# Output projection of a fused attention and FFN kernel: bias rows through ScalarE instead of a matmul

## The reference, cut to what matters

```
x : [128, 64, 128]   ctx : [128, 64, 128]        (8192 tokens of width 128; 16 heads of width 8)
k = ctx @ Wk.T + bk ;  v = ctx @ Wv.T + bv ;  q = layernorm(x) @ Wq.T + bq
attn = softmax(k.q / sqrt(8)) over the 64 keys ;  out = attn applied to v
x = x + (out @ Wo.T + bo)                        # the output projection that is changed
h = layernorm(x)
3 times:  y = lin(gelu(layernorm(lin(h)))) ;  h = y + h      # dequantised weights plus low rank parts
x = x + h
```

## Time and profile before

| | |
|---|---|
| median of 3 runs | 371.1 us (370.62 to 373.37) |
| the profiled execution | 371.78 us |
| its span in the trace | 370.0 us, mean granted clock of TensorE 0.986 |
| instructions | 13066 |

### The profile page before, as it was taken

One profiled execution on the slowest core, in us unless ns is written; L12 is line 12 of the kernel. 1 busy time (PEld: TensorE's weight loads), 2 busy tenths in 40 slices (PEclk: granted clock), 3 DMA queues, 4 the chain that ended last, 5 costly groups with the idle time before them and its releaser, 6 DMA issues.

```text
span 370.0 us, 13066 instructions
## 1 busy us (share of the span) xinstructions
PE 342.1 (92%) x4797; PEld 256.4 (69%) x4797; DVE 334.4 (90%) x834; ACT 285.0 (77%) x575; POOL 268.6 (73%) x265
## 2 busy tenths in 40 slices
PE   7778999999999999999979785989999999999985
PEld 5355567677667766776756563776788888888874
DVE  5897999999999999999999999769999999988762
ACT  4567888788878878887867445558999999999983
POOL 4555678888877987788788878857787778784231
PEclk9989999999999999999999998799999999999999
DMA  7994476568547754864661400000011000100112
GB/s 191 245 275 135 135 233 205 156 183 244 175 134 213 211 162 139 253 194 144 176 198 73 131 4 2 3 0 0 3 31 58 28 28 28 59 29 30 57 31 85
DMA packets 54514, 43.29 MB, mean 117 GB/s; under 512 B 4608, under 2 KB 48592, under 8 KB 54480
## 3 DMA queue, kind: packets, MB, share of 16 engines
q1 hardware_dynamic: 53904, 42.31, 38.4%
q10 hardware_dynamic: 576, 0.53, 0.5%
HBM read 26.05 MB, written 16.78 MB: 116 GB/s over the span
## 4 chain that ended last, share of the span: by engine, by line
PE 65%; DVE 21%; issue 5%; ACT 5%; DMA 1%; POOL 1%; DVEq 0%; ACTq 0%; POOLq 0%
PE score_ps L1468 10%; DVE negmax L746 6%; PE att_ps L1444 6%; DVE zsum L760 6%; PE score_ps L1375 6%; PE wo_ps L1224 5%; PE score_ps L1236 4%; PE score_ps L1536 3%; PE work L1529 3%; PE work L1260 3%; PE att_ps L1536 3%; PE score_ps L1462 3%; PE work L1273 3%; PE work L1266 2%; PE work L1254 2%
## 5 line engine op out<-in xcount | busy, mean ns | idle before, releaser
L492 POOL TENSOR_TENSOR probs<-probs,rz 128x1024 f32<-128x1024 f32 x64 | 136.3, 2139 | 35.4 <-DVE rz L763 35.2
L503 POOL TENSOR_TENSOR rs<-ve,minus_half 128x4 f32<-128x4 f32 (+1 forms) x50 | 59.3, 1186 | 42.1 <-DVE ve L700 30.7
L1017 ACT ACTIVATE probs<-score_ps 128x1024 f32<-128x1024 f32 x64 | 65.6, 1024 | 22.9 <-PE score_ps L1375 22.4
L760 DVE TENSOR_REDUCE zsum<-probs 128x64 f32<-128x1024 f32 x64 | 77.3, 1208 | 1.5 <-ACT probs L1017 1.3
L746 DVE TENSOR_REDUCE negmax<-score_ps 128x64 bf16<-128x1024 f32 x64 | 75.2, 1177 | 1.7 <-PE score_ps L1236 1.7
L1375 PE MATMUL score_ps<-negmax,ident_bf 128*128 128x512 bf16 x128 | 39.2, 388 | 8.4 <-DVE negmax L746 8.3
L1468 PEld LDWEIGHTS score_ps<-lin_t,h 128*128 128x128 f32 x312 | 38.7, 195 | 11.7 <-DVE h L823 6.3
L1224 PEld LDWEIGHTS wo_ps<-wo_t,att_t 128*128 128x128 f32 x256 | 36.8, 191 | 13.7 <-issue 12.1
L1073 ACT ACTIVATE z<-score_ps,rs 128x128 f32<-128x128 f32 x156 | 44.7, 382 | 1.0 <-POOL rs L503 1.0
L1444 PE MATMUL att_ps<-probs,v_diag 128*32 128x64 f32 x2048 | 43.5, 224 | 0.7 <-POOL probs L492 0.6
L1468 PE MATMUL score_ps<-lin_t,h 128*128 128x128 f32 x312 | 41.6, 281 | 2.5 <-ACT probs L1017 1.1
(11 more groups left out here) (215 smaller groups left out, 680.9 us busy)
## 6 DMA issues: line engine op xcount, KB each, us to landing
q_parts<-parts SPq DMA_DIRECT2D x15, 512.0 KB, 3.5
k_stack<-k_parts SPq DMA_DIRECT2D x30, 256.0 KB, 3.3
q_stack<-q_parts SPq DMA_DIRECT2D x60, 128.0 KB, 2.8
ctx_sb<-in_ctx SPq DMA_DIRECT2D x16, 256.0 KB, 3.6
k_parts<-parts SPq DMA_DIRECT2D x16, 256.0 KB, 2.8
out<-x_all SPq DMA_DIRECT2D x15, 256.0 KB, 2.3
x_all<-in_x SPq DMA_DIRECT2D x14, 256.0 KB, 3.8
x_all<-in_x SPq DMA_DIRECT2D x1, 512.0 KB, 5.6
```

Of the source, the lines that this page charges most:

```text
L492: nc.gpsimd.tensor_tensor(e[:, :, :, :], e[:, :, :, :], by_query.broadcast_to([P, BANDS, SEQ, ADJ]), ALU.mult).then_inc(s_probs, 1)
L503: nc.gpsimd.tensor_tensor(rs2[v][:, lo:hi], ve2[v][:, lo:hi], minus_half[:, lo:hi], ALU.pow).then_inc(p_rs[v], 1)
L760: nc.vector.tensor_reduce(zsum[q][:, :], probs[(p - 1) % 4][:, :, :, :].rearrange("p u k s -> p k u s"), AX_XY, ALU.add).then_inc(s_zsum, 1)
L1017: nc.scalar.activation(probs[p][:, :, :, :], score_ps[p % 2][:, :].rearrange("p (u s k) -> p u k s", s=ADJ, k=SEQ), ACT.Exp, scale=SCALE). ...
```

## The change

The bias matmul of the output projection is taken out. In chunk 1 an extra matmul of 256 columns (PE, slot 1) puts the bias row on all partitions into the free half of `wo_ps`, and ScalarE copies 128 columns of it into a new SBUF tensor `bo_rows`. From then on `projection_seed(k)`, a ScalarE copy of `bo_rows`, four times side by side, into the 512 columns of `wo_ps`, stands in place of the bias matmul. It is issued right behind the exponential of slot 0 in chunk k + 2 (k = 14: at the end of slot 3 of chunk 15; k = 15: in slot 2 of chunk 16, behind the exponential's place) and waits for `s_x2`. PE issues pieces 0 and 1 in slot 0 of chunk k + 2, piece 2 in slot 1, piece 3 in slot 2 and none in slot 3, and waits in slot 0 for `att_t` and for the copy (`s_wo_seed`). The matmuls accumulate onto what ScalarE wrote. For chunks 14 and 15 all four pieces are in slot 0 of chunks 16 and 17.

```diff
--- before.py
+++ after.py
@@ -137,6 +137,7 @@
         zsum = [sb(f"zsum{i}", [P, SEQ]) for i in range(2)]
         rz = [sb(f"rz{i}", [P, SEQ]) for i in range(4)]
         att_t = [sb(f"att_t{i}", [P, 2, CHUNK // 2]) for i in range(2)]
+        bo_rows = sb("bo_rows", [P, D])
 
 
         st2 = [None] + [sb(f"st2_{v}", [P, 2 * TPC if v == 1 else TPC, 6]) for v in range(1, 4)]
@@ -213,6 +214,7 @@
         s_v = sem("s_v")
         s_att_t = sem("s_att_t")
         s_wo = sem("s_wo")
+        s_bo, s_wo_seed = sem("s_bo"), sem("s_wo_seed")
         s_x2 = sem("s_x2")
 
         s_scores = sem("s_scores")
@@ -679,6 +681,7 @@
                 nc.vector.tensor_tensor(res_cols[:, 1:2], cols[:, ROW_BL + 3:ROW_BL + 4], cols[:, ROW_BL + 5:ROW_BL + 6],
                                         ALU.add).then_inc(s_seed, 1)
                 dve.wait_ge(s_seed_ps, 1)
+                dve.wait_ge(s_bo, 1)
                 raw = wo_ps[:, 2 * P:4 * P].rearrange("p (v d) -> p v d", v=2)
                 nc.vector.tensor_reduce(seed_sum[:, :], raw, AX_X, ALU.add).then_inc(s_seed, 1)
                 dve.wait_ge(s_seed, 2)
@@ -975,6 +978,16 @@
                 src = k_dram[0].rearrange("(g r) l t -> (r l) g t", g=GROUPS)
                 for a in range(2):
                     act.dma_start(k_stack[0][a:P:2, :, :], src).then_inc(h_k_stack, 16)
+
+            def projection_seed(k):
+
+                if isinstance(k, int) and k == 0:
+                    act.wait_ge(s_seed, 4)
+                    act.wait_ge(s_bo, 1)
+                if some(k):
+                    act.wait_ge(s_x2, k)
+                nc.scalar.activation(by_token(wo_ps[:, :]), bo_rows[:, :].unsqueeze(1).broadcast_to([P, TPC, D]),
+                                     ACT.Copy).then_inc(s_wo_seed, 1)
 
             def prologue():
                 bias_loads()
@@ -1020,6 +1033,8 @@
 
                 if live(c):
                     exponentials(0)
+                if live(c - 2) and live(c):
+                    projection_seed(c - 2)
                 if isinstance(c, int) and c == 0:
                     act.wait_ge(s_v_ps, 1)
                     act.wait_ge(s_vzero, 2)
@@ -1036,6 +1051,9 @@
                 if live(c + 2):
                     q_high(c + 2, par)
                     q_low(c + 2, par)
+                if isinstance(c, int) and c == 1:
+                    act.wait_ge(s_seed_ps, 1)
+                    nc.scalar.activation(bo_rows[:, :], wo_ps[:, 0:P], ACT.Copy).then_inc(s_bo, 1)
                 early_steps("ACT", c, 1, step)
 
                 if live(c - 1):
@@ -1051,6 +1069,8 @@
                     k_low(c + 2, par)
                 if isinstance(c, int) and c == 0:
                     transposed_layers(0)
+                if isinstance(c, int) and c == NCHUNK:
+                    projection_seed(NCHUNK - 1)
                 early_steps("ACT", c, 2, step)
 
                 if live(c):
@@ -1062,6 +1082,8 @@
                     if live(c - 1):
                         act.wait_ge(s_pv, PPC * c)
                     value_blocks(c + 1, 1 - par)
+                if isinstance(c, int) and c == NCHUNK - 1:
+                    projection_seed(NCHUNK - 2)
                 early_steps("ACT", c, 3, step)
 
             def normalise(v, k, lo, count, src):
@@ -1214,6 +1236,8 @@
                 for v in range(2):
                     nc.tensor.matmul(wo_ps[:, P * (2 + v):P * (3 + v)], pick_row[:, 3 + v, :], bias3[:, :], start=v == 0,
                                      stop=v == 0, skip_group_check=True)
+                nc.tensor.matmul(wo_ps[:, 0:2 * P], pick_row[:, 1, :], bias3[:, :].unsqueeze(1).broadcast_to([P, 2, P]),
+                                 start=False, stop=False, skip_group_check=True)
                 nc.tensor.matmul(wo_ps[:, 3 * P:4 * P], neg_last[:, :], lin_t[:, 4, :], start=False, stop=True,
                                  skip_group_check=True).then_inc(s_seed_ps, 1)
 
@@ -1406,23 +1430,18 @@
 
                     if isinstance(c, int) and c == NCHUNK - 1 and p == 3:
                         step(3, 1)
-                    if p == 3 and live(c - 1):
-                        pe.wait_ge(s_att_t, c)
-                        if some(c - 1):
-                            pe.wait_ge(s_x2, c - 1)
+                    if live(c - 2):
+                        if p == 0:
+                            pe.wait_ge(s_att_t, c - 1)
+                            pe.wait_ge(s_wo_seed, c - 1)
+                        if isinstance(c, int) and c >= NCHUNK:
+                            pieces = range(TPC) if p == 0 else ()
                         else:
-                            pe.wait_ge(s_seed, 4)
-                        bias_rows(wo_ps[:, :], 1)
-                        project_out(0, att_t[1 - par])
-                    if isinstance(c, int) and c == NCHUNK:
-                        if p == 0:
-                            for t in range(1, TPC):
-                                ins = project_out(t, att_t[par])
-                            ins.then_inc(s_wo, 1)
-                    elif p < 3 and live(c - 2):
-                        ins = project_out(p + 1, att_t[par])
-                        if p == 2:
-                            ins.then_inc(s_wo, 1)
+                            pieces = ((0, 1), (2,), (3,), ())[p]
+                        for t in pieces:
+                            ins = project_out(t, att_t[par])
+                            if t == TPC - 1:
+                                ins.then_inc(s_wo, 1)
 
                     mc, mp = (c, p - 2) if p >= 2 else (c - 1, p + 2)
                     if live(mc):

```

## The result

The changed kernel takes 404.35 us (median of 4 runs, 402.98 to 406.0) against 372.11 us (4 runs, 370.62 to 373.37) of the kernel before beside it: ratio 1.0889, 95% interval 1.0842 to 1.0935. The forecast was 392.0 with a range of 386 to 397: right in the direction, 12 us too low. The profiled execution took 405.15 us, its span is 403.3, 33.3 more than before.

The account below looks back on a forecast made before the run. The prediction took PE to bound the loop, with no idle time, and DVE close behind at 1.6% idle. Its terms, 18.8 + 1.6 + 0.7 + 0.3 - 0.5 = 20.9 us, on 371.1 gave 392.0, range 386 to 397.

Parts of the forecast that it names:

- The walk: One loop period followed on ACT and PE: PE stalls 1.85 us in slot 0 for the copy, period 14.37, longer by 1.71.
- rival 2: Gaps bring TensorE's clock down to 0.66 in the loop: 6.4 us more per period, some 460 us; chance 0.03.
- chunks 2 to 12, at full clock: Eleven loop periods up to chunk 12's slot-3 shift, each 1.71 us longer: 18.8 us more.
- chunk 13: Slot 0: copy lands 2.30 us behind the shift against 0.88, plus a second piece; DVE backlog hides a little: 1.6 more.
- chunk 14: Slot 0: copy and pieces delay the next shift, its exponential done 212.67 where DVE started the sum at 211.97: 0.7 more.
- up to chunk 1's slot 3: In chunk 1 the `bo_rows` copy, 128x128, stands ahead of the exponential of slot 2: 0.3 us more.
- behind chunk 14: Chunk 15 adds 0; in chunks 16 and 17 two bias matmuls of 0.22 us leave the path: 0.5 us less.
- Rival 1: PE wins back 0.1 us per slot, 0.4 per chunk, from small gaps: 4.4 less, 387.6 us; chance 0.14.
- Rival 3: The copy is on ACT before PE reaches the pieces, so hidden; DVE is the limit: 2.7 less, 368.4 us; chance 0.03.
- Rival 4: PE alone sets the time all through and ACT costs nothing: 4.8 us less, 366.3; chance 0.01.

Follow-up runs that it names:

- copy_early: Changed kernel with ScalarE's bias-row copy moved behind the exponential of slot 3 of the chunk before, ahead of the normalised input: 372.0 us, ratio 1.0025.
- pieces_slots_1_2: Changed kernel with projection pieces 0 and 1 in slot 1, 2 and 3 in slot 2, TensorE waiting for the copy in slot 1: 377.01 us, ratio 1.0169.
- fill_stall: Also experiment 1: changed kernel with the context transposes done four times more ahead of TensorE's slot-0 wait, chunks 2 to 13: 395.53 us, ratio 1.0671.
- wait_longer: Kernel before plus two useless ScalarE copies behind the slot-0 exponential and TensorE's wait for them ahead of piece 1: 408.75 us, ratio 1.1058.
- pieces_last: Changed kernel with the two slot-0 pieces moved behind the input transposes, the slot's last work; copy and wait stay: 379.87 us, ratio 1.0217.
- wait_alone_b: Kernel before plus one useless ScalarE copy into SBUF behind the slot-0 exponential and TensorE's wait for it ahead of piece 1: 392.48 us, ratio 1.0609.
- fill_1_b: Changed kernel with the context transposes done once more in slot 0 ahead of TensorE's wait: 396.87 us, ratio 1.0708.

## Why the prediction was right or wrong, point by point

**The walk was right.** Forecast and measured from the slot-3 shift on: slot-0 shift 2.68 and 2.73, slot-0 exponential 3.83 and 3.93, copy 4.75 and 4.86, pieces 5.41 and 5.60, slot-1 shift 7.95 and 8.20, slots 1 and 2 together 6.42 and 6.41, period 14.37 and 14.61; the stall 1.85 and 1.82; the copy 0.60 and 0.596. Three small terms make the 0.24: the exponential starts 1.20 behind the value blocks, not 1.10 (they have no overlap there), the hop from the copy to TensorE took 0.14 and not 0.06, and two pieces took 1.06 and not 1.0. The copy's price by the rule of the Trainium skill (ScalarE: Activation LUTs, Rules for kernel authors), 0.73, was an estimate without the rule's condition: its 0.3 us are for an ACTIVATE whose bias is a pointer operand, and this copy is given no bias.

**The step that failed** is rival 2 and its argument against: "from 203 to 217, busy 10.67 of 14 (76%), it stayed at 1.00, and the new period is busier". A busy share over a stretch was taken for what holds the clock, and so the sum has the clock at nothing. In the stretch 120 to 163 the changed kernel was busy 37.19 of 43.00, 86%, and the clock was 0.95; copy_early had shares of 74% at 1.00 in its last chunks (11.06 of 15.00 us from 210 to 225). What went with the falls in the loop was how TensorE's idle time lay: in one stall of 1.8 us or more in a chunk. That is no rule for the whole kernel. In copy_early one idle time of 2.85 us left the clock at 1.00 (from 186 to 193 us):

```profile
189.65 0.60 PE L1397 MATMUL score_ps<-negmax,ident_bf 128*128 128x512 bf16 x2 [2.85 <-DVE negmax L749]
```

And in pieces_slots_1_2, in chunk 14, three shorter ones close together (0.92, 0.61 and 0.56 us) stood ahead of a fall; the shift at 214.72 already takes 1.03 instead of 0.60, and the granted clock from there to 218.00 is 0.50:

```profile
211.92 0.61 PE L1399 MATMUL score_ps<-negmax,ident_bf 128*128 128x512 bf16 x2 [0.92 <-DVE negmax L749]
...
213.74 0.42 PE L1260 MATMUL score_ps<-q_stack,k_stack 64*64 64x128 f16 x16 [0.61 <-ACT probs L1030]
214.72 1.03 PE L1399 MATMUL score_ps<-negmax,ident_bf 128*128 128x512 bf16 x2 [0.56 <-DVE negmax L749]
```

The price was wrong too: it was worked out as a clock low all the time, 70 us, while each fall lasted some 3 us and cost 1.3. A rival that can come in part, once in two chunks, has to be priced per event and put into the range. With the price measured here a fall in each of the eleven passes is 11 x 1.3 = 14.3 us, so the range would have reached from 392.0 to 406, with the 404.35 in it.

**The sum, term by term** (spans of the profiled executions; the full-clock terms from fill_stall, the clock as what the changed kernel has more than it):

```
                                   forecast   measured
chunks 2 to 12, at full clock        18.8       21.2    (160.46 against 139.24)
chunk 13                              1.6        1.4    (16.08 against 14.72)
chunk 14                              0.7        0.5    (13.57 against 13.11)
up to chunk 1's slot 3                0.3        1.0    (0.74 of it ahead of any changed instruction)
behind chunk 14                      -0.5       -1.4    (153.02 against 154.45)
clock, chunks 2 to 12                 0          6.9    (167.35 against 160.46)
clock, chunks 13, 14 and behind       0          3.8    (1.3 + 1.5 + 1.1)
sum                                  20.9       33.3
```

(The lines have more digits than they show, so they add up to 33.4.) Of the 12.4 missed, 10.7 are the clock against fill_stall, and 9.7 against the kernel before: behind chunk 14 that kernel has a fall of its own (0.66 from 226 to 236 us) and fill_stall has none, so the -1.4 in that line is in part the clock, and the two lines behind chunk 14 together, -0.3, are near the -0.5 forecast. Most of the rest, 2.4, is the period of 14.6 instead of 14.37. That the last 3.8 are the clock's is argued, not shown: fill_stall has its filler in chunk 13 as well, but in chunk 14 both kernels run the same instructions, and from 238 to 250 us the changed one has a clock of 0.86, fill_stall 1.00.

The Trainium skill (TensorE: Matmul & The Clock Gate, HAM oscillation) describes a matmul kernel whose wait in every pass of its loop sends the clock down again and again. The traces agree in part: the granted clock is 0.52 from 131.0 to 134.3 us, and the long periods recur in the changed kernel and in wait_longer. But it is not every pass: five of eleven, and seven of eleven. The remedy there, not to let TensorE wait between bursts, is experiment 1 in its crudest form.

**The other rivals.** Rival 1 (TensorE wins back in slots 1 and 2): not in the changed kernel, 6.41; in pieces_last these slots took 6.28 (123.43 to 129.71), as the input copy was ready early. Rivals 3 and 4 (a faster kernel): excluded by the result. Rival 3's condition, though, was the right one: a copy queued ahead of the value blocks is hidden, and the time is then that of the kernel before. Its price, 2.7 less, was too good: the loop gained 11 x 12.66 - (184.69 - 46.73 = 137.96) = 1.3 us, and chunk 13 took 0.7 of it back. Rival 4 falls with that too. By the rule of the Trainium skill (Perfetto Trace Analysis, Identifying Performance Opportunities) the most contended engine is the one to relieve. The prediction took TensorE for it by the busy share of its matmuls, 92%. But the same section calls that share a poor measure for TensorE and names, beside the arithmetic done against the peak, the busy share of its weight loads. By that, 69% against DVE's 90%, DVE was the engine to relieve, and the rule did not speak for the change. The trace agrees: taking 0.3 us a chunk off TensorE gave nothing that could be measured even in copy_early, where its wait was gone, and there DVE held the chain.

## What to carry to other kernels

When work moves to an engine with room, the room is a total; what counts is when the new instruction comes up in that engine's queue and how soon the busy engine needs it. Walk one period from the trace with both queues side by side: it gave the new period within 0.25 us here. And where the change leaves TensorE standing still inside a loop, put a fall of its clock into the range as a price per event, times the passes of the loop; a busy share of 86% is no safety.

## What the runs showed of the hardware that was not expected

- Stalls and clock, in the loop of the profiled executions: 0.8 us (pieces_last), 1.3 (wait_alone_b) and 1.5 (fill_1_b) left it at 1.00 in every chunk; 1.8 (wait_longer) brought it down in seven chunks of eleven. In the changed kernel it fell in five, behind a stall of 1.97 each time, and not behind the other six of 1.8 to 1.95. The kernel before had one idle time of 2.05 us, at 192 us, and copy_early one of 2.85, and both stayed at 1.00. So a stall of this length can bring it down, and need not. With a longer stall the busy share of the microseconds around it falls too, and no run separates the two. That in the changed kernel it was each second chunk stays open.
- These counts rest on one execution each. In wait_alone_b the mean granted clock over the span was 0.987 in the profiled execution (389.23 us) and 0.972 in the slowest (394.59), and no trace shows where the clock of that one fell.
- TensorE went on 0.14 us after the end of a ScalarE copy into PSUM (129.93 to 130.07), 0.05 after one into SBUF of the same size (123.31 to 123.36 in wait_alone_b).
- Useless matmuls in front of a wait made a kernel 9 us faster.
